# Moving the first two context tiles ahead of the first two attention tiles in a cross-attention stage

## What is computed

```python
def _L0_xattn_ref(x, W_qkv, W_o, beta_q, beta_k, gate, log_tau, K_mem, V_mem, clip_k):
    Q = (x @ W_qkv.T)[..., :D]
    coef = (alpha * beta_q + (1.0 - alpha) * beta_k) * scale * tau
    scores = coef * jnp.einsum('bsd,bnd->bsn', Q, K_mem)
    scores = scores - jnp.max(scores, axis=-1, keepdims=True)
    thr = jax.lax.top_k(scores, clip_k)[0][..., -1:]
    scores = jnp.where(scores < thr, -jnp.inf, scores)
    att = jax.nn.softmax(scores, axis=-1)
    out = jnp.einsum('bsn,bnd->bsd', att, V_mem)
    return out @ W_o.T
x = _layernorm(x + _L0_xattn_ref(x, ..., ctx_2048, ctx_2048, 54), axis=-1)
```

## Time and profile before

| what | value |
|---|---|
| runs | 1660.25, 1669.37, 1671.63 us; median 1669.37 |
| the profiled execution | 1660.18 us |
| its span, first to last instruction | 1658.4 us |
| mean granted PE clock, share of full speed | 0.937 |
| busy: PE, DVE, ACT, POOL | 1472.2, 1192.4, 908.1, 776.3 us |
| instructions | 27698 |

### The profile page before, as it was taken

How to read it: one execution, slowest core, us unless ns; L and a number is a source line. 1 busy time by engine, 2 the same in 40 slices (tenths; PEclk the granted TensorE clock), 3 DMA queues, 4 the chain that set the end, 5 groups by cost and what they waited for, 6 DMA issues and landing times.

```text
span 1658.4 us, 27698 instructions
## 1 busy us (share of the span) xinstructions
PE 1472.2 (89%) x10404; PEld 902.0 (54%) x10404; DVE 1192.4 (72%) x2027; ACT 908.1 (55%) x1463; POOL 776.3 (47%) x685
## 2 busy tenths in 40 slices
PE   6798878887778889587999999999999999999984
PEld 2366656576634444242555665566556665666553
DVE  3776796978359999948866776766676677667757
ACT  3367675665545544455465556545655565556542
POOL 3744351721223214868554465446644564556412
PEclk9989997997599999778999999999999999999997
DMA  9500010003010210210000100110010001001002
GB/s 291 201 26 2 28 52 29 26 16 114 27 51 26 77 52 1 64 64 13 26 26 26 39 26 26 33 32 26 26 39 26 26 26 39 26 26 39 1 1 102
DMA packets 68149, 74.68 MB, mean 45 GB/s; under 512 B 9009, under 2 KB 46513, under 8 KB 66993
## 3 DMA queue, kind: packets, MB, share of 16 engines
q1 hardware_dynamic: 67440, 68.68, 12.8%
q10 hardware_dynamic: 576, 4.19, 0.7%
HBM read 49.66 MB, written 10.49 MB: 36 GB/s over the span
## 4 chain that ended last, share of the span: by engine, by line
PE 67%; DVE 15%; issue 9%; ACT 5%; POOL 2%; SPq 1%; DMA 0%; DVEq 0%; ACTq 0%; POOLq 0%
PE banks L1145 49%; PE banks L902 7%; PE banks L1009 2%; DVE nmf L1527 2%; PE banks L993 2%; PE banks L972 2%; PE banks L956 1%; ACT pf L1235 1%; DVE top L1651 1%; DVE wk L1647 1%; DVE attf L1658 1%; PE banks L974 1%; PE banks L995 1%; PE banks L1100 1%; ACT kcT L1186 1%
## 5 line engine op out<-in xcount | busy, mean ns | idle before, releaser
L1145 PE MATMUL banks<-xc,w 128*128 128x512 f16 x2688 | 591.9, 383 | 18.1 <-ACT banks L1186 15.1
L1145 PEld LDWEIGHTS banks<-xc,w 128*128 128x128 f16 x2688 | 264.5, 99 | 340.0 <-ACT banks L1186 20.3
L1145 PE MATMUL banks<-wd,mid 128*128 128x256 f16 x2688 | 298.1, 273 | 5.7 <-ACT banks L1186 3.1
L1145 PEld LDWEIGHTS banks<-wd,mid 128*128 128x128 f16 x2688 | 263.5, 98 | 41.3 <-ACT banks L1186 3.4
L879 POOL TENSOR_TENSOR mid<-m,mid 128x512 f16<-128x512 f32 x64 | 75.1, 1173 | 319.6 <-ACT mid L1186 319.6
L1186 ACT ACTIVATE banks<-banks 128x512 f32<-128x512 f32 x192 | 108.6, 578 | 192.7 <-PE banks L1145 192.7
L879 POOL TENSOR_TENSOR mid<-msum,mid 128x512 f16<-128x512 f32 x128 | 185.9, 1471 | 2.6 <-ACT mid L1186 2.6
L1474 DVE SCALAR_TENSOR_TENSOR w<-stage,w 128x512 f16<-128x512 f32 (+1 forms) x56 | 61.4, 1135 | 106.1 <-ACT w L1186 106.1
L1186 ACT ACTIVATE mid<-msum 128x512 f16<-128x512 f32 x128 | 81.0, 633 | 84.5 <-DVE msum L1832 28.2
L1527 DVE TENSOR_REDUCE nmf<-banks 128x1 f32<-128x512 f32 (+3 forms) x256 | 107.2, 480 | 21.8 <-PE banks L974 21.2
L779 POOL TENSOR_TENSOR plo<-pf,phi 128x1280 f16<-128x1280 f32 x24 | 63.2, 2640 | 118.1 <-ACT phi L1186 117.7
(11 more groups left out here) (256 smaller groups left out, 2987.5 us busy)
## 6 DMA issues: line engine op xcount, KB each, us to landing
stage<-w_fold SPq DMA_DIRECT2D x24, 256.0 KB, 3.0
stage<-in_Wg SPq DMA_DIRECT2D x24, 256.0 KB, 3.1
stage<-in_Wu SPq DMA_DIRECT2D x24, 256.0 KB, 3.1
stage<-in_Wd SPq DMA_DIRECT2D x24, 256.0 KB, 2.8
vcat<-vnext SPq DMA_DIRECT2D x8, 528.0 KB, 3.4
x_in<-in_x SPq DMA_DIRECT2D x4, 1024.0 KB, 6.5
x_res<-in_x SPq DMA_DIRECT2D x4, 1024.0 KB, 5.6
c_raw<-in_ctx SPq DMA_DIRECT2D x4, 1024.0 KB, 5.6
```

What stands on the lines that cost most here:

```text
L1145: mm = nc.tensor.matmul(out, l(x, i), r(y, i), start=start and i == 0 and j == 0, stop=stop and i == k - 1 and j == 2, skip_group_check=True)
```

## The change

In the sequences of a full step cT.0 and cT.1 move from behind aT.1 (on PE) or aT.0 (on ACT) to the front. The same transposes, copies and roundings are issued, in another order. The sequences of DVE, POOL and SP, the banks and all buffers stay as they are. The last step stays too.

```diff
 B_BODY_PE = steps("""
-    aT.0 aT.1 cT.0 cT.1 xT.0 cT.2 cT.3 out.0 xT.1 A.0 A.1 A.2 A.3 aT.2 out.1 aT.3 out.2 out.3 sc.0 xT.2 sc.1
+    cT.0 cT.1 aT.0 aT.1 xT.0 cT.2 cT.3 out.0 xT.1 A.0 A.1 A.2 A.3 aT.2 out.1 aT.3 out.2 out.3 sc.0 xT.2 sc.1
     xT.3 CW.0 sc.2 CW.1 x2.0 x2.1 x2.2 CW.2 sc.3 CW.3 x2.3
 """)
 B_BODY_ACT = steps("""
-    aT.0 cT.0 cT.1 cT.2 cT.3 A.0 top.2 aT.1 A.1 xT.0 top.3 A.2 aT.2 aT.3 xT.1 A.3 ln.0 sc.0 sc.1 xT.2 xT.3 x2.0
+    cT.0 cT.1 aT.0 cT.2 cT.3 A.0 top.2 aT.1 A.1 xT.0 top.3 A.2 aT.2 aT.3 xT.1 A.3 ln.0 sc.0 sc.1 xT.2 xT.3 x2.0
     x2.1 first.0 CW.0 sc.2 CW.1 first.1 x2.2 CW.2 CW.3 x2.3 sc.3
 """)
```

## The result

The changed kernel takes 1679.21 us (median of 13 runs, 1672.78 to 1684.73), the kernel before 1669.37 (median of 13, 1659.6 to 1674.32). The ratio is 1.0081, 95% interval 1.0061 to 1.0102: slower by 0.8%, some 10 to 17 us, 13.5 by the ratio. The forecast was +12.8 and 1678.2.

The account below looks back on a forecast made before the run. The prediction took DVE, with next to no gaps in the full steps of cross attention, as the bound. DVE's delays of 8.3 us plus 4.5 for PE's clock gave +12.8, put on a mean of 1665.4: 1678.2 us, range 1664 to 1688.

Parts of the forecast that it names:

- The bank wait: Second and third full step: cT.1 waits for x2.3's bank, making DVE's low half of aT.0 3.1 and 3.0 us late.
- The first step: First full step: cT.1's copy waits for POOL's low half of CW.3, making DVE's low half of aT.0 2.2 us late.
- the first term: DVE's delay at the low half of aT.0, summed over the three full steps: 2.2 + 3.1 + 3.0 = 8.3 us.
- The clock: PE's longer wait before aT.2 lowers its clock over out.1 to out.3: 1.5 us per full step, 4.5 in all.
- that overlap at the x2 tiles: POOL's low half of cT.0 beside DVE's low halves of x2: taken as nothing; by attf's row 2 us more.
- Giving nothing back: Before A.0 and aT.2: earlier context halves only lengthen PE's wait for attf; 0 us back, bounds 0 and 2.6.
- the last paragraph of the prediction: Signs in the profile after, among them the step from aT.0 to aT.0: some 61.8 us, or 60.3 without the fall.
- the clock stays up: Rival: same DVE delays, but PE's longer wait before aT.2 costs no speed; +8.3 us, 1673.7; chance 0.25.
- Long falls: Rival: behind aT.2 each full step loses 2.7 us to the clock; +16.4 us, 1681.8; chance 0.13.
- Not slower: Rival: PE, not DVE, sets the pace, so an earlier A.0 counts; -2.6 us, 1662.8; chance 0.06.
- A delay made up inside the step: Rival: DVE's own gaps of some 3 us per step take up half the delay; +4 us, 1669.4; chance 0.06.
- The forecast by the mean of four executions: Whole kernel: the 12.8 us added to 1665.4, the mean of four known executions lying in two places, giving 1678.2.

Follow-up runs that it names:

- the hybrid: Changed kernel with cT.1 in bank 5 and, in the first full step, only cT.0 ahead of aT.0; stretch 233.71 us, ratio 1.0007 to before.
- the hybrid with extra matmuls: The hybrid plus unused PE matmuls before aT.2, eight in the first full step, four in the other two; median 1665.10 us, ratio 0.9977 to before.

## Why the prediction was right

**The bank wait.** Predicted from the earlier trace rows: DVE's low half of aT.0 late by 3.1 and 3.0 in the second and third step. Measured: gaps of 3.04 us and 3.04 us. Moving cT.1 to bank 5 takes both away with everything else left as it is. The working was right to the path: the transposes of aT.0 were hidden behind ACT's pair.

**The first step.** Predicted 2.2 from the earlier trace rows, through copyf and POOL's low half of CW.3. Measured against the first CW product: 15.40 (519.23 - 503.83) where before has 13.35, 2.05 late. The size is right, the reason only in small part. ACT in after:

```profile
515.98 0.60 ACT L1186 ACTIVATE copyf<-banks 128x512 f32<-128x512 f32 x1 [0.27 <-PE banks L1073]
...
517.45 0.60 ACT L1186 ACTIVATE copyf<-banks 128x512 f32<-128x512 f32 x1 [0.15 <-POOL cw L798]
...
518.62 0.58 ACT L1186 ACTIVATE attT<-banks 128x512 f16<-128x512 f32 x1
```

POOL's low half took its 1.63 again, and ACT waited 0.15 us for it. By then ACT was just done with cT.0's pair; without POOL the copy could have begun at some 517.2 (an estimate: 516.67 + 0.54). What holds attT is ACT's own four operations. That the two paths end within 0.25 us of each other, so that the wrongly named one gave the right number, is luck. The sum of the first term was 8.3; it is 8.1 (2.05 + 3.04 + 3.04).

**The clock.** Predicted 1.5 in each step, 4.5, with bounds 0 and 2.7. DVE's waits for out.t grew by 6.0 in all. The extra matmuls in PE's wait took 6.2 of them away (8.2 to 2.0), and 5.6 us of the stretch. So the term is 5.6, more than I took and inside the bounds. By DVE's low half of aT.0 in one step and the next, after against the kernel with extra matmuls, the first step paid 2.27 (62.57 against 60.30), since the whole of out.1 lay in the fall (5.02 us); the second paid 1.69 (61.63 against 59.94), and the rest of the stretch 1.65 (104.32 against 102.67). For the second and third I had the wait before aT.2 too long: 2.05, not 2.8 to 3.8. The wait grew less than DVE's delay because PE's own work ahead of A came later too: in the second step A began at 587.23, only 1.6 us earlier against DVE's low half of aT.0 than in before (5.43 us behind it in place of 7.02). That even 2.05 was enough for a fall I had not derived. Both executions of the changed kernel had it, but the hybrid and the repeated runs show that such a wait can go either way. That the falls came behind waits this short is the part of the forecast that its rows didn't carry.

**What was left out.** 8.1 + 5.6 is 13.7, and the stretch grew by 12.65. The missing 1.1 came back at attf, and the chain of after has a part of it; it answers to the fourth of the earlier trace rows:

```profile
598.91 1.41 DVE attf L1658 x4
```

It was 1.69 there. The largest part is in the third step. Before:

```profile
637.40 1.16 POOL L798 TENSOR_TENSOR kq<-copyf,kq 128x512 f16<-128x512 f32 x1 [1.44 <-ACT kq L1186]
637.61 1.49 DVE L1658 SCALAR_TENSOR_TENSOR attf<-tsc,top,ex 128x512 f32<-128x512 f32 x1
```

In after POOL's low half of that A tile is over at 659.38 and the same attf, at 660.53, took 0.73. With 0.28 in the second step and 0.15 in the first that is 1.2 in all. So before, POOL's low half of A.2 ran beside attf; in after A ends earlier against DVE. DVE being late isn't needed for it. With cT.0 alone ahead, where DVE has no gap in the third step:

```profile
649.21 1.16 POOL L798 TENSOR_TENSOR kq<-copyf,kq 128x512 f16<-128x512 f32 x1 [1.43 <-ACT kq L1186]
...
650.53 0.73 DVE L1658 SCALAR_TENSOR_TENSOR attf<-tsc,top,ex 128x512 f32<-128x512 f32 x1
```

I had weighed that overlap at the x2 tiles, where it cost nothing: xc took 2.47 again, with POOL at work on cT.0's low half until 577.40. I had not looked for overlaps that the move would end. By the Trainium skill (GPSIMD Engine Reference, Specifications) DVE instructions with two SBUF inputs contend with POOL; attf, which has them, agrees with 1.49 against 0.73, and xc, which reads a bank, with 2.47 against 2.47.

**Giving nothing back.** Predicted 0, since an earlier A only lengthens PE's wait. On PE that is so: with bank 5 the wait before aT.2 grew from 0.70 to 1.71 and 1.81, and one of the two brought a fall, which cost 1.7 us (58.49 for that step, against 56.81 in the hybrid, where it had none). But the 1.1 us at attf are given back by the earlier A, through POOL. In the hybrid with extra matmuls DVE is 0.6 late in the first step, nothing falls, and the three parts of the stretch behind that are 0.2, 0.4 and 0.75 us shorter than in before. So what was said of PE's wait holds, and POOL beside DVE's attf was overlooked; 1.1 lies in the bounds of 0 and 2.6.

**How good the 12.8 was.** It is 0.15 from the stretch's 12.65 by two errors that cancel: the clock was taken 1.1 too small, and what comes back 1.1 too small as well. The first term, 8.3 against 8.1, makes up the rest. One slip is in the last paragraph of the prediction: 57.3 + 3.1 + 1.5 is 61.9, not 61.8, and without the fall 60.4, not 60.3.

**The rivals.** That the clock stays up (+8.3) is out by the windows. Long falls (+16.4) are out: no step paid 2.7. Not slower is out; PE waited for attf in every step, and DVE, not PE, set the pace. The rival has a grain of truth: the one version that is not slower needs cT.1 off bank 1, as that rival had it, and what it gains comes of an earlier A, though by DVE's attf and not by PE's wait. A delay made up inside the step is out: the steps grew from 57.3 and 57.2 to 62.6 (581.80 - 519.23) and 61.6. The forecast by the mean of four executions, 1665.4 + 12.8, was luckier than its two ends: the scatter of the runs was not explained, only averaged. The median of before turned out at 1669.37, and with 12.8 on it the time would be 1682.2, 3.0 above the measured one.

## What to carry to other kernels

When a part is moved forward in a hand-written order, look up what its buffer was last used for: the gap that it is to fill may end later for it than for the work that it passes, and every engine that follows a strict order passes the wait on. A gap on an engine that the chain doesn't go through is in itself no gain to be had, and making that engine ready earlier lengthens its wait for the engine that is the bound; where the early engine is PE, the longer wait can cost the clock at the moment when its result is needed. What moves with it counts too: look for operations on other engines that now run beside the bound, or no longer do. To judge a few us in a kernel whose runs scatter by 15, measure between two landmarks around the change, and take a second profile before trusting 3 us.

## What the runs showed of the hardware

- PE's granted clock fell behind waits of 1.23 us (0.50 from 649 to 651 us in PE's order alone), 1.71, 1.80, 2.05 and 2.41 us, and did not behind others of 1.23, 1.81, 2.13, 2.15 and 2.40. The same place in two executions of one kernel came out both ways (1.23 in the third step; 2.12 and 2.13 in the first). The twelve matmuls of out.1 took 2.75 us at full clock and 4.05 to 5.24 with a fall.
- Eight matmuls of no use (1.89 us) in a wait of 3.65 kept the clock at 1.00 and, with the same in the two other steps, made the stretch 5.6 us shorter. The Trainium skill (TensorE: Matmul & The Clock Gate, HAM oscillation) has a kernel whose matmuls run at half rate behind each wait and an order of work that avoids the waits; the trace agrees as to the cost, with 4.44 against 2.75 us for the same matmuls.
- A 128x512 f32 SCALAR_TENSOR_TENSOR of DVE with two SBUF inputs (attf) took 0.73 us alone and 1.49 and 1.68 us with a POOL operation on SBUF beside it.
- The stretch of the changed kernel repeated to 0.02 us in two executions that reached it 4 us apart, and that of bank 5 to 0.00; that of PE's order alone differed by 3.0, by falls of the clock that came once and not again. What lies ahead of it scattered by 12.5 over the traces.
